# A fused decoder layer: output projection four units forward, weights on ACT's queue, reciprocal row sums spread over partitions by DMA through DRAM

## What is computed

```python
q, k = rope(LN(x) @ Wq.T), rope(LN(x) @ Wk.T);  v = LN(x) @ Wv.T     # 32, 8 and 8 heads of 64
attn = softmax(where(causal, q @ k.T / 8, -max));  x = x + concat(attn @ v) @ Wo.T   # Wo: 256 x 2048
# scan: state = state*exp(delta*A) + delta*u*B ; y = sum over 16 n of state*C ; y = y + D*u
x = x + swapaxes((y * silu(z)))                    # z = LN(x), 4 batches of 256 channels x 256 steps
x = x + (silu(LN(x) @ Wgate) * (LN(x) @ Wup)) @ Wdown                # 704 hidden, int32 weights
```

## Time and profile before

| | us |
|---|---|
| median of 3 runs (444.4 to 446.76) | 446.46 |
| the profiled execution | 442.86 |
| its span in the trace | 441.1 |
| PE busy | 386.5 |
| DVE busy | 347.4 |
| ACT busy | 268.9 |

### The profile page before, as it was taken

How to read it: one execution, slowest core, us unless ns; L and a number is a source line. 1 busy time by engine, 2 the same in 40 slices (tenths; PEclk the granted TensorE clock), 3 DMA queues, 4 the chain that set the end, 5 groups by cost and what they waited for, 6 DMA issues and landing times.

```text
span 441.1 us, 7761 instructions
## 1 busy us (share of the span) xinstructions
PE 386.5 (88%) x2636; PEld 309.3 (70%) x2636; DVE 347.4 (79%) x479; ACT 268.9 (61%) x775; POOL 181.5 (41%) x262
## 2 busy tenths in 40 slices
PE   4789987788899989997899889988989899699997
PEld 3546776566787868776777667766867677488885
DVE  1865758597898999899889978998997998485532
ACT  2356799366776767666667666765663768633221
POOL 2742443246456354635463536353551544121000
PEclk9989999899999989999999999999999899999999
DMA  9852258365664759496647593966458753200000
GB/s 226 167 103 49 61 125 275 97 192 125 154 130 149 145 136 245 122 226 146 143 152 143 134 225 71 220 140 164 130 117 188 188 111 62 49 1 25 25 25 24
DMA packets 55287, 57.42 MB, mean 130 GB/s; under 512 B 32840, under 2 KB 43280, under 8 KB 55248
## 3 DMA queue, kind: packets, MB, share of 16 engines
q1 hardware_dynamic: 40672, 32.84, 27.2%
q0 software_dynamic: 9792, 22.10, 24.7%
q10 hardware_dynamic: 4784, 1.99, 1.8%
HBM read 26.36 MB, written 1.18 MB: 62 GB/s over the span
## 4 chain that ended last, share of the span: by engine, by line
PE 42%; DVE 19%; issue 17%; DMA 9%; POOL 7%; ACT 4%; SPq 1%; DVEq 0%; ACTq 0%; POOLq 0%
PE ps_p L1083 9%; PE ps_so L1100 7%; DMA y<-state 6%; PE ps_p L1314 5%; PE ps_so L1297 5%; DVE nmax L740 5%; PE ps_r L1152 4%; PE ps_p L1198 4%; DVE state L820 3%; POOL rc L427 3%; ACT prob L505 3%; PE ps_so L1180 2%; POOL qt L270 2%; DVE state L833 2%; PE ps_so L1111 2%
## 5 line engine op out<-in xcount | busy, mean ns | idle before, releaser
L505 ACT ACTIVATE prob<-ps_so,nmax 128x256 f32<-128x256 f32 (+1 forms) x256 | 104.7, 441 | 50.0 <-DVE nmax L740 50.0
L427 POOL TENSOR_TENSOR rc<-rc,rs 128x512 f32<-128x512 f32 x40 | 58.4, 1460 | 110.5 <-DVE rs L728 76.0
L511 ACT ACTIVATE pt<-ps_r 128x512 f32<-128x512 f32 x96 | 53.7, 593 | 40.6 <-PE ps_r L1152 40.6
L1083 PE MATMUL ps_p<-xt_all,wq 128*128 128x256 f32 x256 | 65.5, 400 | 10.9 <-ACT vv L489 4.8
L827 DVE TENSOR_TENSOR_SCAN state<-decay,state 128x1024 f32<-128x1024 f32 x32 | 73.3, 2291 | 1.1
L740 DVE TENSOR_REDUCE nmax<-ps_so 128x2 f32<-128x512 f32 (+1 forms) x96 | 60.2, 683 | 16.2 <-PE ps_so L1111 16.1
L270 POOL DMA_DIRECT2D qt<-rc x128 | 64.8, 519 | 10.0 <-POOL rc L427 9.5
L1083 PEld LDWEIGHTS ps_p<-xt_all,wq 128*128 128x128 f32 x256 | 47.4, 195 | 24.8 <-issue 6.4
L1198 PE MATMUL ps_p<-wo,attn_t 128*128 128x256 f32 x256 | 60.0, 381 | 5.0 <-DVE x L850 5.0
L434 POOL DMA_DIRECT2D y<-state x32 | 29.8, 930 | 73.4 <-DVE state L833 71.2
L1100 PE MATMUL ps_so<-kt,qt 64*128 64x256 f32 (+1 forms) x512 | 52.7, 347 | 8.2 <-DMA qt<-rc 4.8
(11 more groups left out here) (108 smaller groups left out, 523.0 us busy)
## 6 DMA issues: line engine op xcount, KB each, us to landing
bc<-bc_scratch SPq DMA_DIRECT2D x32, 512.0 KB, 4.9
y<-state POOLq DMA_DIRECT2D x32, 512.0 KB, 5.8
qt<-rc POOLq DMA_DIRECT2D x128, 32.0 KB, 2.1
qt<-rc SPq DMA_DIRECT2D x128, 32.0 KB, 2.3
wo<-wo_t SPq DMA_DIRECT2D x1, 2048.0 KB, 14.5
wq<-wqkv_t SPq DMA_DIRECT2D x28, 64.0 KB, 2.5
kt<-kt SPq DMA_DIRECT2D x7, 256.0 KB, 3.0
kt<-rc POOLq DMA_DIRECT2D x34, 32.0 KB, 1.8
```

The lines of the kernel that those rows point to most:

```text
L427: nc.gpsimd.tensor_tensor(rc[:, r % 2, :, :], rc[:, r % 2, :, :], rs[:], ALU.add).then_inc(rope_add, 1)
L505: nc.scalar.activation(o, i, ACT.Exp, bias=nmax[:, r, c:c + 1], accum_out=rsum[:, r, GRP + head:GRP + head + 1]).then_inc(exp_done, 1)
L511: nc.scalar.activation(pt[:, fill, :], ps_r[:, fill % 2, :], ACT.Copy).then_inc(pt_copied, 1)
L1083: last = nc.tensor.matmul(o, lhs, rhs, start=(k == 0), stop=(k == KT - 1))
```

## The change

Three things change.

1. **Reciprocal sums.** `widen`, `replicate` and `copy_rep` are gone. `turn_sums(u)` is one transpose of the 128x8 reciprocals into 8 rows, and stands behind the scores of unit u+1. `copy_sums(u)` copies these 8x128 values from PSUM to SBUF on ACT, ahead of the exponentials of unit u+1. `spread_sums(u)` is on SP, behind `move_q(u+2)` and, where they occur, `double_k`, `load_wq`, the write of `bc_scratch` and (in unit 2) the first `load_bc`: SP waits for `copy_sums`, writes 4 KB to a DRAM scratch, waits until they have landed, and issues two DMAs of 128 KB that read each row back over 64 partitions into `rep_s`. `scale_attn` waits for these. The later loads and moves on SP stand behind it.
2. **Output projection.** Pair g of batch b now stands in unit 8*b+g+4, one in each of units 4 to 27; units 28 to 30 take two each of the last batch, pair 6 stands behind the last unit's first transposes and pair 7 at the very end. `add_attention(b)` stands at the start of DVE units 12, 20 and 28.
3. **Loads of weights.** Wo comes in 8 DMAs of 256 KB, two at the end of ACT's units 1 to 4, the feed-forward weights in 11 more on ACT's queue in units 5 to 10, 13 and 14.

```diff
-LAST_PAIRS = {UNITS - 4: (0,), UNITS - 3: (1, 2), UNITS - 2: (3,)}
+WO_LAG = 4
+WO_PAIRS = {8 * b + g + WO_LAG: ((b, g),) for b in range(B - 1) for g in range(KVH)}
+WO_PAIRS.update({UNITS - 4 + i: ((B - 1, 2 * i), (B - 1, 2 * i + 1)) for i in range(3)})
...
+            def spread_sums(u):
+
+                r = u % 2
+                sp.wait_ge(sums_copied, u + 1)
+                if u >= 2:
+                    sp.wait_ge(rep_in[r], 16 * 2 * (u // 2))
+                sp.dma_start(sums_dram[r].rearrange("o (c s) -> (o c) s", s=P), sums(u)).then_inc(sums_out[r], 16)
+                sp.wait_ge(sums_out[r], 16 * (u // 2 + 1))
+                if u >= 2:
+                    sp.wait_ge(attn_copied, u - 1)
+                for odd in range(2):
+                    sp.dma_start(rep_s[odd * HD:(odd + 1) * HD, r, :],
+                                 sums_dram[r, odd:odd + 1, :].to_broadcast([HD, 4 * P])).then_inc(rep_in[r], 16)
...
-                if u == 2:
-                    sp.dma_start(wo[:], wo_t.rearrange("(k p) n -> p k n", p=P)).then_inc(wo_in, 16)
-                load_ffn(u)
+                spread_sums(u)
...
-            def widen(u):
...
-            def copy_rep(u):
-
-                act.wait_ge(rep_done, u + 1)
+            def copy_sums(u):
+
+                act.wait_ge(sums_done, u + 1)
                 if u >= 2:
-                    act.wait_ge(attn_copied, u - 1)
-                nc.scalar.activation(rep_s[:, u % 2, :], ps_r[:, 1, :], ACT.Copy).then_inc(rep_copied, 1)
+                    act.wait_ge(sums_out[u % 2], 16 * (u // 2))
+                nc.scalar.activation(sums(u), ps_r[0:2 * GRP, 1, 0:P], ACT.Copy).then_inc(sums_copied, 1)
...
+            def load_weights(u):
+
+                if 1 <= u <= 4:
+                    for g in (2 * u - 2, 2 * u - 1):
+                        nc.scalar.dma_start(wo[:, 2 * g:2 * g + 2, :], wo_t[2 * g * P:(2 * g + 2) * P, :].rearrange(
+                            "(k p) n -> p k n", p=P)).then_inc(wo_in[g], 16)
+                elif u in (5, 6):
+                    nc.scalar.dma_start(wgu_i[:, u - 5, :], wgate_t[(u - 5) * P:(u - 4) * P, :]).then_inc(ffn_in, 16)
...
-                dve.wait_ge(rep_copied, u + 1)
+                dve.wait_ge(rep_in[u % 2], 16 * 2 * (u // 2 + 1))
...
+                if u >= KVH + WO_LAG and u % KVH == WO_LAG:
+                    add_attention(u // KVH - 1)
                 if u + 2 < UNITS:
                     rope(("q", u + 2))
...
-                if u in (2 * KVH, 3 * KVH):
-                    add_attention(u // KVH - 2)
-                if u == UNITS - KVH // 2:
-                    add_attention(LAST - 1)
...
-            def replicate(u):
...
+            def turn_sums(u):
+
+                pe.wait_ge(rinv_done, u + 1)
                 pe.wait_ge(pt_copied, u * 3 + 2)
...
+                nc.tensor.transpose(ps_r[0:2 * GRP, 1, 0:P], rinv[:, u % 2, :], ident[:]).then_inc(sums_done, 1)
```

More of the change, by code:

```diff
@@ L162, in decoder_layer @@
         xdbl = attn_t[:].rearrange("p a s -> p (a s)")[0:XR, 3 * L:4 * L]
[L164 to L167, removed]
+        sums_first = wgu[:].rearrange("p w k n -> p (w k n)").bitcast(F32)[0:2 * GRP, 0:2 * P].rearrange(
+            "p (r s) -> p r s", r=2)
+        sums_later = x1[0:2 * GRP, LAST * TB, :].rearrange("p (r s) -> p r s", r=2)
+        sums = lambda u: (sums_first if u < KVH else sums_later)[:, u % 2, :]
         raw = prob0[:].rearrange("p a b s -> p (a b s)")
@@ L186, in decoder_layer @@
         ps_p = ctx.enter_context(nc.psum_tensor("ps_p", [P, 2, 512], F32))
-        ssm_in, tab_in, wo_in, ffn_in = (sem(n) for n in ("ssm_in", "tab_in", "wo_in", "ffn_in"))
+        ssm_in, tab_in, ffn_in = (sem(n) for n in ("ssm_in", "tab_in", "ffn_in"))
+        wo_in = [sem(f"wo_in{g}") for g in range(KVH)]
         x_in = [sem("x_in0"), sem("x_in1")]
@@ L230, in decoder_layer @@
         rope_add = sem("rope_add")
-        wide_done, rep_done, rep_copied = sem("wide_done"), sem("rep_done"), sem("rep_copied")
+        sums_done, sums_copied = sem("sums_done"), sem("sums_copied")
+        sums_out = [sem(f"sums_out{r}") for r in range(2)]
+        rep_in = [sem(f"rep_in{r}") for r in range(2)]
         decay_done = sem("decay_done")
@@ L1153, in transpose_p @@
                 last.then_inc(pt_done, 1)
-            def replicate(u):
-                pe.wait_ge(wide_done, u + 1)
+            def turn_sums(u):
+                pe.wait_ge(rinv_done, u + 1)
                 pe.wait_ge(pt_copied, u * 3 + 2)
-                for pair in range(GRP // 2):
-                    for t in range(TB):
-                        c = t * GRP + 2 * pair
-                        src = rwide(u)[:, c:c + 2, :].rearrange("p o k -> p (o k)")
-                        last = nc.tensor.transpose(ps_r[:, 1, pair * S + t * P:pair * S + (t + 1) * P],
-                                                   src, ident[:])
-                last.then_inc(rep_done, 1)
+                nc.tensor.transpose(ps_r[0:2 * GRP, 1, 0:P], rinv[:, u % 2, :], ident[:]).then_inc(sums_done, 1)
             def values(u):
@@ L1186, in values, with out_project @@
                 last.then_inc(pv_done, 1)
-            def out_project(b, pairs):
-                for pair in pairs:
+            def out_project(*pairs):
+                for b, pair in pairs:
+                    if b == 0:
+                        pe.wait_ge(wo_in[pair], 16)
                     if b == 0 and pair == 0:
-                        pe.wait_ge(wo_in, 16)
+                        pe.wait_ge(xt_sb, B)
                     if b and pair == 0:
@@ L1247, in unit @@
                 transpose_p(u, 2)
-                replicate(u)
                 if 1 <= u < B:
                     transpose_x(u)
-                if b == LAST and g >= KVH // 2:
-                    out_project(LAST, LAST_PAIRS[u])
-                elif b == LAST:
-                    out_project(b - 1, (2 * g, 2 * g + 1))
-                elif b:
-                    out_project(b - 1, (g,))
+                out_project(*WO_PAIRS.get(u, ()))
                 values(u)
```

81 lines of the change are left out of this document (36 added, 45 removed).

## The result

The changed kernel took 480.1 us, the median of 5 executions, against 446.8 for the kernel before. The ratio is 1.063, with a 95% interval of 1.056 to 1.070. A median takes in all executions, a ratio leaves out those over 1.5% above the fastest of the same kernel, so 480.1 over 446.8 is not 1.063. In one of the 5 executions, the profiled one, a matmul took about four times as long (1729 ns instead of 437 in the queries' projection) and the whole 2118 us. There it took 476.5 us against 447.9 (ratio 1.057, 1.046 to 1.067), and the span of its profiled execution is 474.2 us against 441.1. The prediction was 440.5 with a range of 430 to 452. The kernel is slower, and by more than the rival that was slower.

A forecast was written before the change was run, and what follows sets the result against it. PE was taken to set 12 of units 5 to 27, DVE 11. Transposes 5.0, sums' way -3.0, start-up -0.5, projection 3.2, scan 1.0 and tail 0.3 gave 6.0 us: 446.5 to 440.5 us, range 430 to 452.

The forecast's parts named there:

- the rival that was slower: The sums' way by DMA becomes the bound if reads land after 4.9 us: 455 us, chance 0.23.
- The transposes (+5.0): Three transposes less on PE, 0.33 us a unit: 4.0 us in 12 units, 1.0 at start and end.
- PE works through it without a gap: Plain unit with one scan step, 9.46 us: taken as set by PE, DVE waiting some 0.7 us.
- The way of the sums: DVE's scale_attn waits for sums moved by DMA: 1.1 us late in unit 8, 0.5 in each of six, minus 3.0.
- the prediction's own formula: Two units take at least the sums' time from unit start plus 7.26 us; with 10.7, 9.0 us each.
- This is no loop: Late sums don't hold up the rope ahead of scale_attn, so lateness doesn't pass from unit to unit.
- Those I leave at nothing: Loads of B and C and moves of keys and queries behind SP's wait: no cost.
- The last sentence of the prediction: Forecast is wrong if SP's queue, waiting twice a unit, brings queries late to the scores; costed at nothing.
- Start-up: Queries' stall in unit 4 goes, 4.3 us won; late sums cost 4.0 in unit 2, 0.8 in unit 1: minus 0.5.
- the third rival: Start-up stays as it is, Wo's pieces delaying the queries as before: 444.8 us, chance 0.15.
- Projection, y and tail: Output projection moved forward wins 3.2 us, fewer scan waits for y 1.0, the tail 0.3.
- The first rival: Sums' way becomes the bound, deciding when the reads take over 4 us: 455 us, chance 0.23.

The follow-up runs named there:

- e1: The changed kernel word for word, measured again against the kernel before: 476.5 us, ratio 1.057.
- e14: e2 once more, measured together with e15: 438.0 us, ratio 0.979.
- e15: e6 once more, measured together with e14: 437.0 us, ratio 0.977.
- e6: Changed kernel without the sums' write, reads and every wait for them; scale_attn multiplies by a constant tile: 437.9 us, ratio 0.979.
- e5: Changed kernel with scale_attn multiplying by a constant tile, waiting for the sums only in the last two units; all DMAs stay: 457.7 us, ratio 1.023.
- e2: Changed kernel with the sums back to the old way, projection forward and weights on ACT's queue kept: 438.6 us, ratio 0.9785.
- e4: Kernel before with only the weights moved to ACT's queue, Wo in eight pieces: 445.0 us, ratio 0.990.

## Why the prediction was wrong

It had 6.0 us won, and e1 lost 28.6 against the kernel before it was measured with. Three steps failed, by 4.0, 10.2 and 19.8 us by the medians, which is 34.0 of the 34.6.

**The transposes (+5.0) failed, by 4 us.** 0.33 us times 12 units was right as PE's work and wrong as time. I had taken "PE works through it without a gap" for "PE sets it". In the plain unit of the earlier trace rows DVE waits only 0.7 us, and the copy for `values` hangs on DVE's maxima, so 0.33 us off PE came back as 0.33 us of waiting. Measured: 1.0 (e14, e15), not to be told from nothing. ACT's lighter and earlier work was costed at nothing, and e6 shows no cost of it.

**The way of the sums failed, by 10 us.** For late sums the prediction had 8.6 us in all: 3.0 in six units, 4.8 in units 1 and 2, and 0.8 in unit 29. Without the wait 18.8 us are gone (e5; 15.0 by the ratios). The step was right in unit 8 to 0.6 us, and wrong in taking the shortest unit for the worst. Its 2.6 us for the reads is below the least that any took (2.7 to 6.0, median 3.0). The write's 2.3 us to the reads were right at the median (2.5) and ran from 1.2 to 5.5; in unit 20 `bc` and the adds into y are in flight beside it. In unit 12 the sums need 13.96 us from the start, not 10.7. By the prediction's own formula, with 7.26 for the rest of the second unit, that is 10.6 us a unit; units 12 and 13 took 12.8 and 12.2. "This is no loop" thus held only at 10.7. Fifteen `scale_attn` waited, 2.1 us each, where the prediction had nine; the thirteen outside units 1 and 2 waited 1.8 us each and not some 0.5.

**"Those I leave at nothing" failed, by 20 us.** It is the step on the moves and loads behind SP's wait. Counting SP's work per unit (10 of some 11 us) shows only that the queue doesn't overflow, not when each entry leaves. The hold, the added 8.5 MB and both together cost 19.8 us (e5 less e6), seen as waits for `bc` and queries. The prediction costed the issues and the latency of the new DMAs, but not what their bytes do to others; that term was missing. The last sentence of the prediction, that it is wrong if SP's queue brings the queries late, names one half of it.

**Start-up: right in its parts.** The stall for queries was to go, 4.3 us. Unit 4 fell from 13.26 to 8.90 in e2, 4.4 us; in e1 only to 10.39, since the sums are late there too. The scores that stood at 3.53 us of waiting have none in the changed kernel:

```profile
93.13 1.58 PE L1111 MATMUL ps_so<-kt,qt 64*128 64x256 f32 x16
```

So the third rival is out. The Trainium skill, "DMA: Bandwidth & Descriptors", section "Issuing engines are not separate DMA queues", says that issuing from several engines saves only the time in which the sequencer issues, which is usually small. The prediction read from this that the stall would stay. In e4 it went, and e4 won 1.0% (2.9 us by the medians, 4.6 by the ratio). The 12.05 us in the earlier trace rows are themselves SP's time of issuing, so the skill's words leave room for it, and only "usually small" doesn't fit this case. Whether the other queue, the eight pieces or their spreading over four units did it, no run separates. Late sums in unit 2 were to cost 4.0 and cost 4.9, in unit 1 0.8 and 1.8.

**Projection, y and tail: right in sum, in part by luck.** Unit 24 won 1.9 (2.5 forecast), unit 25 0.7 (0.7), and unit 28 won 0.65 instead of losing 0.6. DVE's waits for y and `bc` fell by 2.5 us in e2 (1.0 forecast). The tail lost 1.4 instead of winning 1.1: from the last `scale_attn` to the end 53.97 us before and 55.34 in e2. Without the sums' terms the prediction comes to 9.6 us (4.3 + 3.2 + 1.0 + 1.1), and e2 won 9.3. But the two profiled executions show only 4.9 of it (442.86 less 437.94). The one before happened to lie 3.6 us under its median, at a granted clock of 0.985 (in the seven beside e2 it was 0.965 to 0.977), and I had taken that to hold afterwards. e2's profiled execution lies 0.6 under its median, so that assumption failed by 3.0 us. The last 1.4 are the other median of the kernel before, 447.9 instead of 446.5. That 9.6 and 9.3 agree is luck by these 4.4 us.

**The first rival named half of the mechanism.** Its time, 455, was too low, since it left the queue and the other transfers as they were. Its condition was that the reads take over 4 us. Over all reads the median is 3.0; but in the fifteen units in which `scale_attn` waited, 3.5 to 6.6 us went by from the start of the first read's issue to `scale_attn`, over 5 in seven of them, where the prediction had 3.2. Its reason against, that small transfers landed in 2.2 to 2.6 us, came from two single transfers of the start-up, not from a unit with its adds into y and its `bc`.

The loss also contains the clock. e1 has the instructions of e6 on PE, but is busy 396.5 us with them against 379.8. This 16.7 us is not added to the above. Where it could be followed, between 282 and 294 us, the lower clock came behind the waits, so it is part of what each undone wait gave back.

## To carry to other kernels

Price a new transfer three times: its own way, what its bytes do to the transfers beside it, and what waits in the queue behind its issue. Take the landing time from rows where the same neighbours are in flight, and look for the unit where they meet, not for the shortest one. An engine without gaps sets a unit only if nobody else is within the saving of setting it too; here 0.33 us off PE needed 0.33 us of slack on the path over DVE's maxima and ACT's copy, which the unit looked at didn't have. Ask first what the change wins if its new cost were nothing; here it was 1 us. The version to keep is e2: the projection forward, the weights on ACT's queue, and the sums on the engines as before, 0.979 of the kernel before.

## What the runs showed of the hardware

- A hand-over through DRAM, a 4 KB write, a wait and two 128 KB reads, took 1.2 to 5.5 us to the read (median 2.5) and 2.7 to 6.0 from there (median 3.0). The Trainium skill, "DMA: Bandwidth & Descriptors", section "Two DMAs through the same engine are not ordered", asks for just this wait, on the first DMA's semaphore before the second is issued. No run here tried without it on the same data.
- Issuing took longer while the DMA engines were full: four moves took SP 2.4 us mostly and 5.11 at 276.30, with a DMA share of 1.01.
- Less PE work did not mean a better clock: with 96 transposes fewer the profiled executions had 0.973 (e6, e15), with them 0.977 and 0.980 (e2, e14).
- One execution of 2118 us, in which DVE's and ACT's busy times were as ever (355 and 245 us) and PE's 2105 us. The granted clock in its records is 1.00, so they don't show what slowed PE. It did not come again, and its cause is open.
